# Cross attention's value product with the values as the stationary operand: 32 array columns for each head, output already transposed

## The reference

```python
x = x + attention(layernorm(x), causal)
q = heads(layernorm(x) @ q_w + q_b)            # 16 heads, 100 x 32
k, v = heads(ctx @ kv_w + kv_b)                # 16 heads, 722 x 32
out = softmax(q @ k.T * 32**-0.5) @ v          # <- the value product
x = x + out.reshape(100, 512) @ proj_w + proj_b
x = x + experts(layernorm(x))
```

## Time and profile before

| | |
|---|---|
| three runs, median | 1271.86 us (1271.14 to 1278.15) |
| profiled execution | 1280.48 us |
| its span, first to last instruction | 1278.7 us |
| PE busy | 1194.4 us, 93% |
| DVE, POOL, ACT busy | 65%, 57%, 50% |
| mean granted TensorE clock | 0.975 |

### The profile page before, as it was taken

One profiled execution on the slowest core, in us unless ns is written; L12 is line 12 of the kernel. 1 busy time (PEld: TensorE's weight loads), 2 busy tenths in 40 slices (PEclk: granted clock), 3 DMA queues, 4 the chain that ended last, 5 costly groups with the idle time before them and its releaser, 6 DMA issues.

```text
span 1278.7 us, 43327 instructions
## 1 busy us (share of the span) xinstructions
PE 1194.4 (93%) x19120; PEld 806.8 (63%) x19120; DVE 830.7 (65%) x1455; ACT 642.2 (50%) x946; POOL 729.6 (57%) x690
## 2 busy tenths in 40 slices
PE   4789899999999999999999999999999877699997
PEld 4456576767667676767676767676767555555543
DVE  4658476858585867676767777677777586423156
ACT  4335556556565656565656464646565535533300
POOL 1436656667676766667675857575757455500042
PEclk9799999999999999999999999999999988799999
DMA  8010611010202010101011110101010345455356
GB/s 302 2 42 2 240 44 50 3 59 3 66 4 65 17 44 9 53 17 52 19 50 32 38 48 12 43 17 52 17 58 11 116 159 190 146 159 170 131 163 212
DMA packets 47840, 93.28 MB, mean 73 GB/s; under 512 B 3775, under 2 KB 15351, under 8 KB 47655
## 3 DMA queue, kind: packets, MB, share of 16 engines
q1 hardware_dynamic: 44135, 79.03, 18.7%
q0 software_dynamic: 3520, 11.47, 2.9%
HBM read 60.13 MB, written 30.36 MB: 71 GB/s over the span
## 4 chain that ended last, share of the span: by engine, by line
PE 86%; DVE 4%; DMA 3%; POOL 3%; ACT 2%; issue 1%; another core or an unknown queue 1%; SPq 1%; ACTq 0%; DVEq 0%
PE psum L323 56%; PE psum L922 7%; PE psum L1025 6%; PE psum L1010 5%; PE psum L940 2%; PE psum L899 2%; PE psum L891 1%; DMA bank<-in_L_attn_Wv 1%; DMA out<-bank 1%; PE psum L967 1%; PE psum L855 1%; PE psum L907 1%; DVE xT L1176 1%; POOL bank L1444 1%
## 5 line engine op out<-in xcount | busy, mean ns | idle before, releaser
L1444 POOL TENSOR_TENSOR bank<-prob,bank 128x1200 f16<-128x1200 f32 x128 | 314.6, 2468 | 188.4 <-ACT bank L1120 188.3
L1268 DVE TENSOR_REDUCE c_most<-psum 100x4 f32<-100x1444 f32 x128 | 211.6, 1653 | 14.7 <-PE psum L1010 12.6
L323 PE MATMUL psum<-bank,cT 128*128 128x512 f16 (+1 forms) x864 | 198.7, 379 | 0.1
L323 PE MATMUL psum<-cT,bank 128*128 128x361 f16 x1152 | 196.1, 321 | 0.0
L1111 ACT ACTIVATE prob<-psum 128x1200 f32<-128x1200 f32 x128 | 150.0, 1172 | 76.6 <-PE psum L1025 62.4
L1176 DVE TENSOR_TENSOR cv<-psum,cv 128x512 f16<-128x512 f32 x125 | 86.0, 688 | 107.4 <-ACT cv L1102 57.2
L1120 ACT ACTIVATE bank<-prob 128x1200 f16<-128x1200 f32 x128 | 151.7, 1198 | 1.4
L323 PEld LDWEIGHTS psum<-cT,bank 128*128 128x128 f16 x1152 | 106.1, 99 | 65.5 <-DVE c_raw L1195 3.0
L323 PEld LDWEIGHTS psum<-bank,cT 128*128 128x128 f16 (+1 forms) x864 | 85.1, 101 | 88.2 <-issue 4.1
L1102 ACT ACTIVATE cv<-psum 128x512 f16<-128x512 f32 x96 | 57.4, 598 | 149.9 <-PE psum L323 148.3
L1229 DVE SCALAR_TENSOR_TENSOR bank<-psum,b_part,bank 128x361 f16<-128x361 f32 x128 | 74.4, 592 | 81.1 <-ACT bank L1088 81.1
(11 more groups left out here) (215 smaller groups left out, 1905.8 us busy)
## 6 DMA issues: line engine op xcount, KB each, us to landing
c_raw<-in_ctx SPq DMA_DIRECT2D x16, 960.0 KB
xs_scratch<-y_kept SPq DMA_DIRECT2D x1, 7424.0 KB, 22.8
c_raw<-xs_scratch SPq DMA_DIRECT2D x29, 256.0 KB, 2.7
ys_scratch<-bank SPq DMA_DIRECT2D x29, 256.0 KB, 2.0
bank<-in_L_ffn_expert_w SPq DMA_DIRECT2D x7, 1024.0 KB, 7.7
x_in<-in_x SPq DMA_DIRECT2D x16, 200.0 KB
x_scratch<-x_out SPq DMA_DIRECT2D x16, 200.0 KB
y_kept<-x_scratch SPq DMA_DIRECT2D x10, 256.0 KB, 3.2
```

Of the source, the lines that this page charges most:

```text
L323: last = pe.matmul(out_ap, a(pa), b(pb), start=(i == 0 and j == 0), stop=(i == len(pairs) - 1 and j == 2))
L1268: dve.tensor_reduce(c_most[:, hf], score[0:L, :, 0:HC], AXIS.X, ALU.max).then_inc(max_done, 1)
L1444: pool.tensor_tensor(prob16[o % 2][:, (2 + part) * PT:(3 + part) * PT], prob[:, part], prob16[o % 2][:, part * PT:(part + 1) * PT], ALU.su ...
```

## The change

`PV` swaps its operands. The values of one head (32 columns, high or low part) are now stationary and the probabilities (100 query columns) moving, and each of the four heads of a group writes 32 partitions of its own: the output is already transposed, head values on partitions. Three passes x 6 tiles x 4 heads = 72 matmuls make the products; 2 x 6 x 4 = 48 more, with a stationary block of ones, make the sums, repeated on the 32 partitions of the head. DVE takes the reciprocal of all 128 x 100 sums and multiplies. `TH`g (ACT) and `TL`g (POOL) split the result of each group straight into `tT`, `scale_heads` and the transposition `TT` are gone, and `TP` waits for the fourth `TL`. In the table, `TP` goes from step 11 (between `SP1` and `SP2`) to the end of step 9 (behind `PV0`, ahead of `A2`); in iteration 14 it goes from step 7 to step 9.

```diff
-    ["MX0", "CX2", "CX3", "rotate_k", "CX4"],
+    ["MX0", "CX2", "CX3", "rotate_k", "CX4", "TH2"],
     ["T0a", "exp0a", "CX5", "PV3"],
-    ["T0b", "SS0", "SS1", "exp0b", "shift0", "scale_heads", "max_A1", "CK0"],
-    ["A1", "CK1", "shift1", "CK2"],
-    ["B1", "high0a", "max_B1", "TT", "low0a", "self_exp0", "SV"],
-    ["MX1", "bias_x", "high0b", "self_sum0", "CV0"],
+    ["T0b", "SS0", "SS1", "exp0b", "shift0", "max_A1", "CK0", "TL2"],
+    ["A1", "CK1", "shift1", "CK2", "TH3"],
+    ["B1", "high0a", "max_B1", "low0a", "self_exp0", "SV"],
+    ["MX1", "bias_x", "high0b", "self_sum0", "CV0", "TL3"],
     ["T1a", "low0b", "SS2", "SS3", "exp1a", "CK3"],
-    ["T1b", "shift2", "PV0", "exp1b", "self_scale0", "shift3"],
+    ["T1b", "shift2", "PV0", "exp1b", "self_scale0", "shift3", "TP"],
     ["A2", "max_A2", "self_scale1", "self_exp1", "self_sum1", "SP0", "CV1"],
-    ["B2", "SP1", "self_scale2", "high1a", "self_scale3", "max_B2", "TP", "high1b", "low1a", "SP2", "SP3",
-     "CV2", "low1b"],
+    ["B2", "SP1", "self_scale2", "high1a", "self_scale3", "max_B2", "high1b", "low1a", "SP2", "SP3",
+     "CV2", "low1b", "TH0"],
...
-    ["T3a", "exp3a", "stats_x", "CQ", "norm_x", "high3a"],
-    ["T3b", "exp3b", "CK7", "split_cq", "PV2", "high3b"],
+    ["T3a", "exp3a", "stats_x", "CQ", "norm_x", "high3a", "TH1"],
+    ["T3b", "exp3b", "CK7", "split_cq", "PV2", "high3b", "TL1"],
...
-    every = [list(step) for step in (moved(STEPS, "TP", 7) if n == B - 2 else STEPS)]
+    every = [list(step) for step in (moved(STEPS, "TP", 9) if n == B - 2 else STEPS)]
...
-                for c in range(HT):
+                def tile(part, t, c):
+                    r = CLAST if t == CT - 1 else CW
+                    at = ((part * 2 + t // 3) * HT + c) * 3 * L + t % 3 * L
+                    return prob16[i % 2][0:r, at:at + L], r
+                for a, (pv, pp) in enumerate(((0, 0), (0, 1), (1, 0))):
                     for t in range(CT):
-                        r = CLAST if t == CT - 1 else CW
-                        for p in range(2):
-                            at = ((p * 2 + t // 3) * HT + c) * 3 * L + t % 3 * L
-                            last = pe.matmul(f[:, c * HV:(c + 1) * HV], prob16[i % 2][0:r, at:at + P],
-                                             cv[odd][0:r, t, HT * i + c, 0:HV],
-                                             start=t + p == 0, stop=t + p == CT)
-            elif name == "TT":
-                pe.wait_ge(c_out_done, it.n)
-                for k in range(KD):
-                    last = pe.transpose(f[:, k * L:(k + 1) * L], c_out[:, k * P:(k + 1) * P], ident[0:L, 0:L])
+                        for c in range(HT):
+                            p, r = tile(pp, t, c)
+                            last = pe.matmul(f[DH * c:DH * (c + 1), 0:L], cv_half[odd][0:r, t, HT * i + c, pv], p,
+                                             start=a + t == 0, stop=a == 2 and t == CT - 1)
+                for pp in range(2):
+                    for t in range(CT):
+                        for c in range(HT):
+                            p, r = tile(pp, t, c)
+                            last = pe.matmul(f[DH * c:DH * (c + 1), L:2 * L], ones16[0:r, 0:DH], p,
+                                             start=pp + t == 0, stop=pp == 1 and t == CT - 1)
...
-                pe.wait_ge(chunk_out, it.done("SO" if name == "OP" else "TT"))
+                    pe.wait_ge(head_split, GROUPS * it.n)
...
+        def act_head_high(act, it, g):
+            n = it.n - 1 if f"TH{g}" in TAIL else it.n
+            act.wait_ge(chunk_out, (its[n + 1] if g == GROUPS - 1 else its[n]).done(f"PV{g}"))
+            act.activation(tT[:, 0, g], head_out[g % 2][:], ACT.Copy).then_inc(head_high, 1)
...
-                heads = f[0:L, 0:HT * HV].rearrange("q (c w) -> q c w", c=HT)
-                dve.tensor_reduce(c_out[:, HT * DH * i:HT * DH * (i + 1)].rearrange("q (c d) -> q c d", c=HT),
-                                  heads[:, :, 0:2 * DH].rearrange("q c (p d) -> q c d p", p=2), AXIS.X, ALU.add)
-                op = dve.reciprocal(c_rinv[:, HT * i:HT * (i + 1)].unsqueeze(2), heads[:, :, 2 * DH:HV])
+                g = GROUPS * (n - 1 if i == GROUPS - 1 else n) + i
+                dve.reciprocal(head_rinv[:], f[:, L:2 * L]).then_inc(head_inv, 1)
+                dve.wait_ge(head_inv, g + 1)
+                if g >= 2:
+                    dve.wait_ge(head_split, g - 1)
+                op = dve.tensor_tensor(head_out[i % 2][:], f[:, 0:L], head_rinv[:], ALU.mult)
...
-        def pool_heads_scale(pool, it):
-            pool.wait_ge(chunk_out, it.done("PV3"))
-            heads = c_out[:].rearrange("q (h d) -> q h d", h=H)
-            pool.tensor_tensor(heads, heads, c_rinv[:].unsqueeze(2).to_broadcast([L, H, DH]), ALU.mult)\
-                .then_inc(c_out_done, 1)
+        def pool_head_low(pool, it, g):
+            count = GROUPS * (it.n - 1 if f"TL{g}" in TAIL else it.n) + g + 1
+            pool.wait_ge(head_high, count)
+            pool.tensor_tensor(tT[:, 1, g], head_out[g % 2][:], tT[:, 0, g], ALU.subtract).then_inc(head_split, 1)
```

More of the change, by code:

```diff
@@ L80 @@
     ["MX3", "X2T", "low2b", "PV1"],
-    ["T3a", "exp3a", "stats_x", "CQ", "norm_x", "high3a"],
-    ["T3b", "exp3b", "CK7", "split_cq", "PV2", "high3b"],
-]
-TAIL = ("low3a", "low3b", "PV3", "scale_heads", "TT", "TP")
-CROSS = tuple(f"{w}{g}" for w in ("A", "B", "max_A", "max_B", "MX") for g in range(GROUPS)) + ("PV0", "PV1", "PV2") + tuple(
+    ["T3a", "exp3a", "stats_x", "CQ", "norm_x", "high3a", "TH1"],
+    ["T3b", "exp3b", "CK7", "split_cq", "PV2", "high3b", "TL1"],
+]
+TAIL = ("low3a", "low3b", "PV3", "TH2", "TL2", "TH3", "TL3", "TP")
+CROSS = tuple(f"{w}{g}" for w in ("A", "B", "max_A", "max_B", "MX") for g in range(GROUPS)) + ("PV0", "PV1", "PV2", "TH0", "TL0", "TH1", "TL1") + tuple(
     f"{w}{g}{p}" for w in ("T", "exp", "high", "low") for g in range(GROUPS) for p in "ab" if w != "low" or g < GROUPS - 1)
-CHUNKS = ("X1T", "X2T", "SQ", "SK", "CQ", "SV", "SO", "OP", "TT", "TP")
+CHUNKS = ("X1T", "X2T", "SQ", "SK", "CQ", "SV", "SO", "OP", "TP")
 CHUNK_KINDS = ("CX", "CK", "CV", "SS", "SP", "MX", "PV", "BV", "FX", "FG", "FW", "FL", "FR", "ST")
@@ L142 @@
 ]
-END_EXTRA = {2: ["PV3", "scale_heads"], 5: ["TT"], 6: ["TP"], 9: ["FS12"], 10: ["FN12"], 11: ["FX12"], 12: ["FL12"],
+END_EXTRA = {1: ["TH2", "TL2"], 2: ["PV3"], 3: ["TH3", "TL3"], 5: ["TP"], 9: ["FS12"], 10: ["FN12"], 11: ["FX12"], 12: ["FL12"],
              13: ["RT10", "RE1"], 14: ["RT11"], 15: ["RT12"], 16: ["RT13"]}
@@ L162, in steps_of @@
     return every
-SPLIT = ("X1T", "SV", "SP0", "SP1", "SP2", "SP3", "SO", "X2T", "TT") + tuple(
+SPLIT = ("X1T", "SV", "SP0", "SP1", "SP2", "SP3", "SO", "X2T") + tuple(
     [f"MX{g}" for g in range(GROUPS)] + [f"CX{c}" for c in range(6)] + ["FG0"] + [f"FW{e}{k}" for e in range(E) for k in range(KD)] + [f"FX{t}" for t in range(TILES)] + [f"CK{c}" for c in range(8)] + [f"CV{c}" for c in range(6)] +
@@ L284, in build_layer @@
         max_sign, max_second, minus = sb("max_sign", [P, 1]), sb("max_second", [P, 1]), sb("minus", [P, P], F16)
-        c_rinv = sb("c_rinv", [L, H])
-        c_out = sb("c_out", [L, D])
+        head_rinv, head_out = sb("head_rinv", [P, L]), [sb(f"head_out{i}", [P, L]) for i in range(2)]
         psum = stack.enter_context(nc.psum_tensor("psum", [P, 8, BANK], F32))
@@ L1070, in act_chunk @@
             act.wait_ge(chunk_ready, it.done(name))
-            if name in ("X1T", "X2T", "SO", "TT"):
-                dst = (xT if name[0] == "X" else oT if name == "SO" else tT)[:, 0].rearrange("p k l -> p (k l)")
+            if name in ("X1T", "X2T", "SO"):
+                dst = (xT if name[0] == "X" else oT)[:, 0].rearrange("p k l -> p (k l)")
                 op = act.activation(dst, f[:, 0:KD * L], ACT.Copy)
@@ L1176, in low @@
                 return dve.tensor_tensor(dst, src, high, ALU.subtract)
-            if name in ("X1T", "X2T", "SO", "TT"):
-                d = xT if name[0] == "X" else oT if name == "SO" else tT
+            if name in ("X1T", "X2T", "SO"):
+                d = xT if name[0] == "X" else oT
                 op = low(d[:, 1].rearrange("p k l -> p (k l)"), f[:, 0:KD * L], d[:, 0].rearrange("p k l -> p (k l)"))
```

32 lines of the change are left out of this document (18 added, 14 removed).

## The result

The changed kernel takes 1351.82 us (median of 4 runs, 1349.72 to 1354.05) against 1272.97 us for the kernel before on the same chip: ratio 1.0613, 95% interval 1.0573 to 1.0652. It is slower, as forecast, but by 79 us where 17 were forecast, and 47 us beyond the top of the range.

A forecast was written before the change was run, and what follows sets the result against it. PE, busy 93% of the span, was taken as the bound. Iterations 1 to 13 +13.8, iteration 0 +0.35, supply +2.5 and the end +0.6 gave +17.2 us: 1296 profiled, 1289 as median, range 1272 to 1305.

The forecast's parts named there:

- `PV`'s own cost: PE's `PV` product: 120 matmuls would take 1.48 us, against 1.46 for the 48 before, so the swap itself earns nothing.
- dearer `PV` per matmul: Rival: `PV` matmuls at 13.5 ns or more, +0.14 x 62 us above the sum; chance 0.13, shared with dearer supply.
- serial loads: Rival: `PV`'s weight loads queue one behind the other, +139 us, 1428 us; chance 0.03.
- `TT` gone, shape changes: PE, each iteration from 1: removing `TT` nets -0.36 us; four `PV` with their shape changes cost +0.22.
- Eviction and `SQ`: DVE's longer eviction of `PV2` delays PE at `SQ` by 0.25 us, 0.12 of it shape change: +0.13 an iteration.
- `TP` moved: PE at `SP2` and `SP3` waits for POOL's scalings once `TP` no longer covers them: 13 x 1.07 = +13.9 us.
- hidden chain: Rival: the chain of scalings before `SP2` and `SP3` stays hidden, so the sum loses 13.9: 1275 us; chance 0.17.
- Instruction supply: PE's 24% more instructions cause one more stop, in iteration 0: +2.5 us, bounds 0 and +10; none in undisturbed iterations.
- more stops for instructions: Rival: PE stops more often for instructions, +7.5 us above the sum; chance 0.13, shared with dearer `PV`.
- the sum: All terms together: +17.2 us on the profiled span of 1278.7, to 1296; chance 0.55.

The follow-up runs named there:

- e1: The changed kernel with `TP` put back in step 11, between `SP1` and `SP2`, nothing else: 1334.5 us, ratio 1.0493.
- e2: The kernel before with `TP` moved to the end of step 9, nothing else: 1289.96 us, ratio 1.0119.
- e3: The kernel before with 72 small matmuls (32 stationary, 4 moving columns) added to every `PV`, each with its weight load: 1352.76 us, ratio 1.0615.
- e5: The changed kernel with `PV` in 72 matmuls instead of 120, same moving columns, and DVE adding the halves first: 1330.25 us, ratio 1.0426.
- e4: The changed kernel with 50 of the 100 moving columns in `PV`'s 120 matmuls, so half the work: 1348.72 us, ratio 1.0583.
- e6: e5 with `TP` put back in step 11: 1317.24 us, ratio 1.0359.

## Why the prediction was wrong

The mechanism was right for `PV`'s own price and for the move of `TP`; one term, the instruction supply, was wrong and makes most of the miss. The direction alone says little for it: `TP`'s move alone or the stops alone would have made the kernel slower. In what follows, iterations are compared matmul by matmul: from the start of one to the start of the next, each step at its median over nine iterations with the same matmuls. By that reckoning an undisturbed iteration takes 62.31 us before, 63.76 after, 62.40 in e1 and 63.53 in e2. So it grew by 1.45 where 1.06 was forecast, and without the move of `TP` the change costs 0.09 (forecast -0.01).

- **`PV`'s own cost:** 1.48 forecast, 1.49 measured. The rivals of dearer `PV` per matmul and of serial loads are out. The pad matmuls of e3 show 8.9 ns for a load and a matmul, so the array has no trouble with this form.
- **`TT` gone, shape changes:** `TP` behind `PV0` takes 2.72, so the price of a shape change holds. But behind `SV` there is a wait that the forecast had at nothing: without `TT` PE comes to `MX1` before the row maxima of `max_B1` are done. From `SV`'s first matmul to `MX1`'s are 2.94 us, 2.59 before. The 0.36 that was to be saved came to about 0.06, 4 us less over 13 iterations. No wait list shows it, since each idle time is under 0.15 us.
- **Eviction and `SQ`:** reciprocal 0.78 us (0.92 forecast), product 0.26 (0.31). `SQ` starts 1.77 us after `PV2` ends, 1.67 before: 0.10 later where 0.25 was forecast, shape change included.
- **`TP` moved:** forecast 13.9, by the earlier trace rows; e1 and e2 show 17.3 and 17.9, in e2's trace 14.8 of them in iterations 1 to 13. The same two waits, 0.42 and 0.29, stand in every one, and `CV3`, two pieces behind them, starts 0.16 later in e2 and in the changed kernel, which the forecast did not have. The view puts the waits down to DVE, as in the earlier trace rows, but POOL's scaling again ends 0.16 before `SP2` starts (604.78 and half of 1.67, against 605.78). The rival of a hidden chain is out.
- **Instruction supply: the step that failed.** The prediction had the count (+24% instructions) and the 16 KB packets, and then argued from the undisturbed iterations of before: "there is no such gap, and it stays so in my sum", +2.5 with a bound of 10. No gap says only that the limit has not been reached, not how far it is. "Issue" rose by 41.0 us in all, 33.2 of them in iterations 1 to 13. What the rows did show is how much the local rate would rise: the chain of before has 48 matmuls of `T` in 0.64 us beside 48 of `PV` in 1.46 (the earlier trace rows for `PV`), and the new `PV` put 120 in the time of those 48. What a block costs in an undisturbed iteration was in no view of before. The two stops of 2.5 us in iteration 0 gave a price under load: from restart to restart 7.27 us, with 127 matmuls between. The rival "more stops for instructions" named the right mechanism, at +7.5 us. The line of before with the 0.64 of `T`:

```profile
634.83 0.64 PE psum L1025 x48
```

- **The miss in numbers:** the sum was +17.2 on the span, the trace has +73.2, so 56.0 are missing. "Issue" is 38.5 of it above the forecast's 2.5. It understates the stops: a matmul is in flight some 0.2 us, and that much of every stop counts as PE busy. From start to start the stops cost 40.1 us more than before in iterations 1 to 13, where the idle time says 33.2. The undisturbed iterations are short by 5.0 (13 times 1.45 against 13.8 forecast), by `TP` and `MX1` above; `SQ` gave a little back. The different beginnings of the two profiled runs are 3.7. A wait of 1.5 at `TP` for `head_out` in one iteration was not forecast either. Together these are 55.6; smaller differences at the beginning and the end, up and down, are not taken apart. The median lies 6.8 us further off than the span, because the profiled run of before was 8.6 above the median that the forecast used and the one after only 1.9.
- **One cost of a stop that is not supply:** behind the stop of 1.77 us at 579.85 `CK0` takes 2.56 us for 9 matmuls and `A1` 1.15 for 12 (usually about 1.5 and 0.67). The window of 581 to 584 us, the last line below, shows why: the granted clock is 0.50, the lower of its two levels, 1.2 GHz, and steps of 0.30 us between matmuls of 361 columns in place of 0.15 fit it. It is the only such stretch in iterations 2 to 13, 3.4 us long, and so costs under 2 us in all.

```profile
579.85 0.20 PE L1032 MATMUL psum<-max_split,minus 32*128 32x100 f16 x1 [1.77 <-issue]
...
580.66 2.56 PE L322 MATMUL psum<-cT,bank 128*128 128x361 f16 x9
583.16 1.15 PE L1017 MATMUL psum<-bank,cq 32*100 32x361 f16 x12
```
```profile
581.10:584.40 3.30, 3.30 (x21) 1.35 (x19) 1.87 (x5) 0.72 (x2) 2.00 (x3) 0.50 0.02 5
```

The Trainium skill's page Runtime: NRT & Kernel Launch (Instruction fetch mechanics) describes blocks of 256 instructions, fetched over a DMA queue of the engine's own, and puts the cost of a block boundary as mostly hidden. The trace agrees with the block and its size. Of some 188 boundaries about 139 were indeed hidden, but the other 49 cost 51.5 us here.

## What to carry to other kernels

When an edit raises the number of instructions on the bound engine, work out instructions per us stretch by stretch, not over the whole span. In this kernel a block of about 256 PE instructions (126 matmuls with their loads) took some 3.8 us to come, so short matmuls that stand one behind the other at 9 to 14 ns each can run PE dry even where the mean demand, 11 blocks in 62 us, is well under the supply. The price to compare with is 3.8 us over 126, 30 ns a matmul. It is not a strict rule: in iterations 1 to 13 the kernel before has stretches of 126 matmuls in 2.81 us and no stop, while the changed kernel's shortest is 1.51. How far ahead blocks are fetched, and so where exactly a short stretch starts to cost, no run here shows. Fewer and longer matmuls with the same columns took the stops away (e5: 39 us of them gone, though its longer eviction gave 21 back), and a stretch without a stop in the trace of before is no proof that there is room. Before moving a piece of PE work, look for what hides behind it: `TP` was the cover of a chain on DVE and POOL, and its move cost 17 us by itself. The same holds for a piece that is removed: `TT` covered a wait at `MX1`.

## What the hardware showed that I had not expected

- When PE waited for two blocks in a row, it restarted 3.65 to 4.00 us apart (twelve pairs in the changed kernel, e1 and e4), whatever the array did in between. While 7.4 MB went to `xs_scratch` it was 7.27 us in the kernel before, and 6.97 and then 5.48 in the changed one; there one stop took 4.72.
- After a stop of 1.77 us the granted clock stood at 0.50 for 3.4 us (changed kernel); most stops of 1.0 to 1.8 us were not followed by such a stretch.
- A matmul of 32 columns with its load costs as little as 8.9 ns when four column strips take turns and the moving operand has 4 columns (e3), and 11.5 with 100 (the sums of `PV`: 48 in 0.55 us); with 50 columns a `PV` fell only from 1.49 to 1.07 us (e4).
- A reciprocal of 100 elements per partition takes 0.78 us on DVE from PSUM and as long from SBUF (e5); that is 6.3 ns for each element beyond the four that took 0.17.
- A product on DVE with both operands in SBUF takes 0.26 us or up to 2.42, by whether POOL's L1461 is under way (e5, e6).
